# Attention b's unrotated score pairs put next to each other, two at a time

## The reference

```
x = x + attn_a(layernorm(x))   # 16 heads of 16, window of 32 and 4 global tokens, softmax
x = x + ffn(layernorm(x))      # silu(x Wg) * (x Wu) -> Wd, hidden 768, int8-like weights
x = x + attn_b(layernorm(x))   # num = exp(q_rot k_rot / 4), den = sum_k exp(q k / 4) over ALL k
x = x + ffn(layernorm(x))      # attn = num/den where causal, else 0
```

## Time and profile before

| | |
|---|---|
| runs shown | 2544.12, 2554.80 and 2557.22 us, median 2554.8 |
| span of the profiled execution | 2536.3 us, first to last instruction |
| its own time | not listed apart; the runs shown lie 7.8 to 20.9 us above its span |
| mean granted TensorE clock | 0.891 |
| busy | PE 82%, PEld 56%, DVE 54%, ACT 57%, POOL 31% |
| `s_bank<-pack_b` L920 | 1024 matmuls, that is 16 sequences x 32 pairs x 2 |
| exponential L1149 | 1024 of 592 ns, and 1024 read-outs of the sum of 193 ns |

### The profile page before, as it was taken

One profiled execution on the slowest core, in us unless ns is written; L12 is line 12 of the kernel. 1 busy time (PEld: TensorE's weight loads), 2 busy tenths in 40 slices (PEclk: granted clock), 3 DMA queues, 4 the chain that ended last, 5 costly groups with the idle time before them and its releaser, 6 DMA issues.

```text
span 2536.3 us, 70747 instructions
## 1 busy us (share of the span) xinstructions
PE 2068.1 (82%) x25221; PEld 1424.4 (56%) x25221; DVE 1375.3 (54%) x2971; ACT 1440.4 (57%) x3580; POOL 793.3 (31%) x1131
## 2 busy tenths in 40 slices
PE   2567788889797888979788897979888898968775
PEld 2345456657464665657465565746566565746444
DVE  3355457565555656465565646556574646545423
ACT  1214656656475655647565664756566565656571
POOL 0013143333433323333333333333333334333321
PEclk7678789989898998989899998989899998979786
DMA  5222423252432324243242425233242524232221
GB/s 147 50 71 61 80 79 76 70 114 59 109 73 79 76 75 104 59 111 71 87 80 78 89 76 115 59 102 80 64 87 70 114 59 116 61 102 44 68 46 38
DMA packets 129715, 202.73 MB, mean 80 GB/s; under 512 B 26768, under 2 KB 60560, under 8 KB 129312
## 3 DMA queue, kind: packets, MB, share of 16 engines
q1 hardware_dynamic: 129344, 197.80, 32.2%
HBM read 67.87 MB, written 51.52 MB: 47 GB/s over the span
## 4 chain that ended last, share of the span: by engine, by line
PE 52%; issue 14%; ACT 12%; DVE 8%; DMA 7%; SPq 5%; POOL 2%; ACTq 0%; DVEq 0%; POOLq 0%
PE gu_bank L1024 14%; PE d_bank L1040 7%; ACT s_bank L1149 5%; PE s_bank L956 5%; ACT probs_B L1139 4%; PE s_bank L920 3%; PE gu_bank L989 3%; PE s_bank L941 3%; SPq L539 3%; DMA xn<-o_scr_B 3%; PE gu_bank L1052 3%; PE gu_bank L999 3%; PE s_bank L907 3%; PE s_bank L787 2%; DMA xn<-o_scr_A 2%
## 5 line engine op out<-in xcount | busy, mean ns | idle before, releaser
L1149 ACT ACTIVATE s_bank<-s_bank 128x512 f32<-128x512 f32 x1024 | 604.6, 592 | 329.4 <-PE s_bank L920 329.1
L1569 POOL TENSOR_TENSOR h<-tmp,h 128x512 fp32r<-128x512 f32 x192 | 246.7, 1285 | 714.8 <-DVE h L1433 711.5
L1139 ACT ACTIVATE probs_B<-s_bank 128x512 f32<-128x512 f32 x640 | 338.2, 606 | 59.1 <-PE s_bank L941 58.7
L1415 DVE SCALAR_TENSOR_TENSOR tmp<-tmp,gu_bank 128x512 f32<-128x512 f32 x192 | 131.2, 683 | 272.8 <-ACT tmp L1178 272.8
L920 PE MATMUL s_bank<-pack_b 48*128 48x512 f16 x1024 | 212.5, 419 | 75.2 <-ACT s_bank L1149 26.0
L1586 POOL TENSOR_SCALAR_AFFINE_SELECT probs_B<-probs_B 128x256 f32<-128x256 f32 x512 | 210.0, 442 | 191.7 <-ACT probs_B L1139 191.7
L1024 PE MATMUL gu_bank<-xT,w_g 128*128 128x256 f32 x1536 | 240.9, 296 | 33.0 <-DVE xT L1408 21.5
L1024 PEld LDWEIGHTS gu_bank<-xT,w_g 128*128 128x128 f32 x1536 | 200.0, 191 | 70.8 <-DVE tmp L1415 23.0
L1024 PE MATMUL gu_bank<-xT,w_u 128*128 128x256 f32 x1536 | 236.3, 293 | 0.4 <-DVE tmp L1421 0.4
L1040 PE MATMUL d_bank<-w_d,h 128*128 128x256 f32 x1536 | 226.0, 291 | 5.2 <-POOL h L1569 4.6
L1040 PEld LDWEIGHTS d_bank<-w_d,h 128*128 128x128 f32 x1536 | 195.6, 190 | 37.3 <-issue 24.2
(11 more groups left out here) (140 smaller groups left out, 3356.3 us busy)
## 6 DMA issues: line engine op xcount, KB each, us to landing
pack_b<-src_b SPq DMA_DIRECT2D x768, 64.0 KB, 2.8
pack_a<-src_a SPq DMA_DIRECT2D x384, 64.0 KB, 2.7
x<-in_L_attn_a_x_dram SPq DMA_DIRECT2D x32, 512.0 KB, 4.0
o_scr_A<-o_raw SPq DMA_DIRECT2D x64, 256.0 KB, 2.4
o_scr_B<-o_raw SPq DMA_DIRECT2D x64, 256.0 KB, 2.1
rden_on<-r_scr_A SPq DMA_DIRECT2D x32, 256.0 KB
xn<-o_scr_A SPq DMA_DIRECT2D x32, 256.0 KB
x_scr<-x SPq DMA_DIRECT2D x16, 512.0 KB, 3.3
```

Of the source, the lines that this page charges most:

```text
L1139: act.activation(probs["B"][:, i, :], score_bank(s, "N", n // 2, n % 2)[:, :], ACT.Exp, scale=SM_SCALE)\
L1149: act.activation(bank[:, :], bank[:, :], ACT.Exp, scale=SM_SCALE, accum_out=den[:, 0, j, 2 * tile + e, t:t + 1]).then_inc(den_exp, 1)
L1569: pool.tensor_tensor(h[1][:, i % 2, :], tmp[:, i % 2, :], h[0][:, i % 2, :].bitcast(F32), ALU.subtract)\
```

## The change

```
     for j in range(GROUPS):
         for q in range(8):
-            put(AT["D"][j] + AT["DS"][j] * q, "D", 8 * j + q, "B")
+            put(AT["D"][j] + AT["DS"][j] * (q - q % 2), "D", 8 * j + q, "B")
```

## The result

The changed kernel takes 2575.8 us (median of four runs, 2564.0 to 2582.0) against 2556.0 us for the kernel before, run beside it on the same chip (four runs, 2544.1 to 2562.5). The ratio is 1.0094, 95% interval 1.0047 to 1.0140: slower by 0.9%, some 24 us. The profiled execution has a span of 2562.0 us, 25.7 above the span of before, and is the lowest of the four runs (2564.03 us).

A forecast was written before the change was run, and what follows sets the result against it. PE was taken as the bound (52% of the chain, busy 128.56 of 148.83 us a slot). +1.8 us in 13 slots is 23, plus about 2 elsewhere: +25 us, median 2554.8 to 2580 us, range 2546 to 2604.

The forecast's parts named there:

- the clock: Rival: granted clock also falls around G 0 in full slots, 1.6 us more a slot, 2601 us; chance 0.14.
- what a couple saves: Two odd pairs adjacent on PE instead of apart: 0.11 us a couple, eight counting couples, 0.9 us a slot.
- The count: Slots the cost applies to: +1.8 us in 13 slots (3 to 15), about 2 us from slots 2, 16 and 17.
- D 11 behind the maxima of A1 3: Ahead of G 0: D 11 waits for maxima that DVE does behind X1, so G 0 starts 1.7 us late.
- G 0 to BV 0: Stretch of a full slot from G 0 to BV 0, foretold to grow by 0.2 us.
- BV 0 behind the maxima of A1 4: Couples 12/13 and 14/15: BV 0 takes A1 4's second bank and comes 0.46 us later relative to A1 4.
- A2 0: Couples 20 to 23: A2 0 takes D 22's first bank, starting 1.25 us after D 22 instead of 0.32.
- D 27 ahead of down 4: Couples 24 to 29: D 27 needs A2 7's bank, delaying down 4; +0.4 us with D 27's old place returned.
- L920's waits for ACT: Sign to look for: L920 gains about 1 us a slot of PE idle time by ACT.
- The next slots have the same length within 0.1 us: Reading of the profile before: one slot of 148.83 us stands for the next ones, so its changes count 13 times.
- a slot at or under 148.8 would make the prediction wrong: Sign against the forecast; the full slot was expected near 150.6 us.
- The third rival: Faster: saved tiling-mode switches count and banks are free, 25 us at most, 2530 to 2541 us; chance 0.12.

The follow-up runs named there:

- eleven semaphore increments: Eleven semaphore increments nobody waits for, ahead of D 11's wait, added to the kernel before with only D 11 moved ahead of G 0; 0.9998 to the kernel before.
- the four couples: Kernel before with only couples 18/19, 20/21, 24/25 and 28/29, whose second pair finds its banks free; run twice, 0.9953 and 0.9955.
- the useless matmuls: Kernel before with five matmuls of 512 bf16 columns, results unread, added behind D 10 and no pair moved; 0.9934, 2534.4 us.
- Five or seven dead matmuls: Unread matmuls ahead of D 11's wait: five in the kernel before with only D 11 moved, 0.9947; seven in the changed kernel, 1.0105 (both to before).

## Why the prediction was right

The sum held: +1.93 us a slot where +1.8 was worked out, +25.7 us of span where +25 was, 2575.8 us where 2580 stood. Not all of its steps did, and that the total came so near is in part luck: a cost that was left out (the clock, 1.1 us a slot) and gains that were too small in the sum or not in it (what a couple saves, the wait behind AV 2) nearly cancel. The count was off as well. Slots 15 to 17 were to add about 3 us and add 0.3, and what lies ahead of slot 3 adds 2.3 where 1 at most was meant.

- **D 11 behind the maxima of A1 3: right, in place, releaser and size.** G 0 was to be +1.7 late; where the clock is whole it is +1.60 (7.88 against 6.28), with PE's wait put on L1307 and none of it left on L1408 in the loop. The steps before it came as reckoned: in the slot shown A1 2 is 2.45 us behind D 8 (reckoned 2.45), X1 5.63 (5.7) and D 11 7.56 (7.7). The experiments bear it out from three sides: alone it costs 0.8%, without it the rest costs nothing, and with ACT as the releaser of the same pair in the same place nothing is lost. The ratios by themselves would not carry this, since eleven semaphore increments move a ratio as far (1.0083 to 0.9998). The stretch from D 8 to G 0 does: 6.28 in before, 7.72 in all slots with D 11 alone moved, with the increments too, 6.44 where only D 11 is back and the clock is whole, and 6.88 with ACT as the releaser.
- **G 0 to BV 0: right without the clock.** +0.2 was worked out and 3.80 against 3.60 measured. The split was too: -0.43 for D 11's old place (foretold -0.3) and +0.57 for BV 0 behind the maxima of A1 4 (foretold +0.46).
- **The clock: left out of the forecast, and there in every slot.** It was a rival with 0.14. In seven of twelve slots G 0 to BV 0 is 4.8 to 5.5, in the other five D 8 to G 0 is 8.4 to 8.7 instead of 7.88. Windows of after, D 8 to G 0 and G 0 to BV 0 of two slots, one with the fall ahead of G 0 and one with it on both sides:

```profile
404.70:413.25 8.55, 5.75 (x66) 3.13 (x65) 6.77 (x16) 6.89 (x18) 1.53 (x4) 0.80 0.50 80
413.25:417.05 3.80, 3.45 (x43) 2.59 (x41) 1.74 (x9) 2.46 (x8) 0.00 (x0) 1.00 0.58 121
699.01:707.91 8.90, 6.25 (x66) 3.15 (x65) 5.77 (x11) 6.92 (x18) 1.53 (x4) 0.66 0.55 94
707.91:713.37 5.46, 5.27 (x43) 4.04 (x41) 1.52 (x9) 2.26 (x6) 0.00 (x0) 0.61 0.60 104
```

  It adds 0.38 us a slot on average to the first stretch and 0.75 to the second, 1.1 of the 1.6 us that the rival named. In the total it is hidden by the next two points. The forecast and this rival were not two cases: both mechanisms ran, and the sum came out near because other terms were smaller than reckoned.
- **What a couple saves: 0.3 us and not 0.11.** The sum counted a pair's own time and not the full-array matmuls beside it (3.91 and 3.59 us above). In N 5 to X of F1 +0.1 was worked out and the table gives -0.13 (22.13 + 2.54 against 21.94 + 2.86); couple 20/21 alone makes 0.2 of that difference. The costs there came as reckoned. A2 0 starts 1.24 us behind D 22 (reckoned 1.25) and waits for its exponential, 0.6 us where 0.7 was foretold:

```profile
1039.40 0.83 PE L835 MATMUL s_bank<-src_a,blocks 128*32 128x508 f16 x12 [0.63 <-ACT s_bank L1149]
```

  X of F1 to AV 2 is unchanged where +0.3 was worked out, and yet D 27 ahead of down 4 (+0.4) is there: with the four couples, which have 24/25 and not 26/27, this stretch is 33.44, and in after 33.75. D 27 costs 0.3, and 24/25 gives 0.3 back where 0.1 was counted.
- **AV 2 to D 28: not foretold.** In 5 of 12 slots the wait put down to issue, the one that goes with the instruction packets, is missing and the stretch 1.5 us shorter; the mean falls by 0.75. In these slots D 28 to the transposes of PB is mostly 8.76 instead of 7.7 to 7.9, so some 0.6 of the 1.5 is kept. The wait was in the trace of before as the longest of L920 and no row of it was weighed.
- **L920's waits for ACT: foretold about 1 us a slot, measured 3** (83.4 against 58.3, and 14 and 11 more for the exponentials of A and B, over 16 sequences). They don't add to the slot one by one, since a wait that is met earlier is missing later.
- **"The next slots have the same length within 0.1 us": wrong.** The twelve slots of before are 142.6 to 148.8 us long; the one that was read was the longest. Nearly all of the spread lies in two stretches, ahead of D 8 (29.2 to 32.9) and at the slot's end (24.0 to 28.4). The granted clock is not whole there: 0.77 in the longest of the former and 0.88 in the shortest, while from D 8 to D 28 it is 1.00 in every one of these slots. The terms were differences inside stretches that do repeat, so the sum was not hurt, but the mark "a slot at or under 148.8 would make the prediction wrong" was: the mean of after is 147.57, and it was an ill-chosen mark.
- **The third rival, saved switches.** It was given 25 us at most, from 0.11 us a couple; the four couples with free banks bring 0.45%, 12 us, and the pairs that wait (11, and BV 0 and A2 0 behind them) lose. The page TensorEngine Tiling (Array Packing) of the Trainium skill, section PSUM Bottleneck, states that tiling speeds up TensorE and not the evacuation of PSUM. This case agrees with it: the exponential that empties a bank takes 592 ns before and 590 after, however its pair is placed.

What stays open: why a few instructions more shorten the written-out slot 0 by 5 us (the windows show that its stops go and that the clock is higher, not which brings the other), and where the rest of the timed gain is. For the useless matmuls 17 us are timed and 9 to 15 are between the profiles; 5 to 8 of these lie ahead of slot 3 and 4 to 7 behind slot 14. That the wait behind AV 2 is one for instructions rests on the packets, which go with it in every slot, and on increments doing what matmuls do; no run delayed or sped up that queue by itself. Nor is it shown where the four couples' 12 us go: their profiled spans are 2536.4 and 2534.7, and the 2536.3 of before is that of a low execution, about 6 and 13 us under the median of before in the two batches that these ratios come from. Single profiles can't place 12 us.

## What to carry to other kernels

Before two pieces are put next to each other on an in-order engine, look up who frees the second one's buffer and what stands ahead of that release in *its* engine's order; a pair that waits for a reducer behind the very operation that the next matmul needs costs the whole distance. Move the pair to a bank that another engine frees, and couple only where the banks are long free. Read several slots before saying what one slot is, and time a variant with a few dead instructions beside any variant that changes the count or order of instructions: here that alone moved the time of two kernels by 0.7 and 0.9%, and that of two others (the four couples, the changed kernel) by nothing that can be told.

## What was not expected of the hardware

- A PE stall of the same length (7.72 us, PE busy for 4.3) left the granted clock whole in seven slots and let it fall to 0.63 in five; a fall cost 1.43 us at this place. Five or seven dead matmuls in the stall kept the clock whole from G 0 to BV 0 in 24 of 24 slots, though in the changed kernel some falls were then ahead of G 0 (D 8 to G 0 up to 10.5 us). In the kernel before, with 6.28 us to G 0, G 0 to BV 0 is 3.60 to 3.62 in 23 of 24 slots.
- A lone 48-row pair between full-array matmuls costs more than its own 0.32 us: the matmuls next to it are 0.1 us slower on either side, so that two pairs next to each other save 0.3 us against two lone ones (D 20 to D 22 3.59 us against 3.91).
- A wait of PE that the profile puts down to "issue" goes with a DMA packet of an instruction queue (q8, 16 KB) that is over 1.2 to 1.6 us before PE starts again: 88 of 88 slots with the wait behind AV 2 have it, and none of the 80 without the wait.
- Eleven semaphore increments, for which nobody waits, took a kernel from +0.83% to -0.02%.
- The timed runs of one kernel lie within 0.7% to either side of the median (2528.4 to 2560.5 and 2542.6 to 2566.4 in two batches of 25 runs of the kernel before), though the means of the stretches from D 8 to AV 2 repeat within 0.04 us.
